# A windowed-attention and convolution kernel: the first MLP product in fp32, the normalised input in a ring of three, and a response stage that lags one strip more

## What is computed

```python
# layer 0, per window of 49 tokens, 3 heads
xn = layernorm(x, norm1)
q, k, v = split(xn @ qkv_w + qkv_b)
attn = softmax(q @ k.T * dh ** -0.5 + bias)
x = x + (attn @ v) @ proj_w + proj_b
h = gelu(layernorm(x, norm2) @ fc1_w + fc1_b)      # 48 -> 192
x = x + h @ fc2_w + fc2_b
# layer 1
y = layernorm(depthwise_conv7x7(x) + dw_b)
y = gelu(y @ w1 + b1)                              # 48 -> 192
gx = sqrt(sum over h, w of y * y)                  # per image and feature
nx = gx / (mean over features of gx + eps)
y = grn_g * (y * nx) + grn_b + y
out = x + y @ w2 + b2
```

## Time and profile before

| | |
|---|---|
| median of 3 runs | 2073.83 us (2071.69 to 2075.19) |
| profiled execution | 2077.34 us, span 2075.7 us |
| mean granted clock of TensorE | 0.946 |
| PE, PE weight loads | 1777.1 us (86%), 1065.6 us (51%) |
| VectorE (DVE) | 1508.5 us (73%) |
| ScalarE (ACT) | 1550.2 us (75%) |
| GpSimd (POOL) | 1174.7 us (57%) |
| first and last of the attention loop's `normalise1` | 80.5 and 1399.4 us |
| first and last output of the response stage | 1734.3 and 2060.2 us |

### The profile page before, as it was taken

The page is one execution under the profiler, slowest core; times in us unless marked ns, Lnnn a source line. Parts: engine busy times, 40 slices in busy tenths (PEclk is TensorE's granted clock), DMA queues, the critical chain, the costliest instruction groups (busy, mean ns, idle before and its releaser), DMA issues. The chain is left out here.

```text
span 2075.7 us, 90932 instructions
## 1 busy us (share of the span) xinstructions
PE 1777.1 (86%) x38074; PEld 1065.6 (51%) x38074; DVE 1508.5 (73%) x2014; ACT 1550.2 (75%) x2882; POOL 1174.7 (57%) x1048
## 2 busy tenths in 40 slices
PE   4989898989888898989898989874999959889884
PEld 2655555555555555555555555531788823223321
DVE  7687777878777777787777777534777757767772
ACT  3788888888888888888888888763566658777770
POOL 4676767777776767676767777731455611111121
PEclk9999999999999999999999999985899957889998
DMA  4334544343434343434434343312587769899983
GB/s 106 80 101 106 146 104 115 91 115 87 119 84 118 86 118 87 109 96 105 100 97 109 93 112 83 93 32 56 155 216 211 203 128 197 218 217 211 242 200 105
DMA packets 233223, 262.18 MB, mean 126 GB/s; under 512 B 167078, under 2 KB 179910, under 8 KB 232710
## 3 DMA queue, kind: packets, MB, share of 16 engines
q1 hardware_dynamic: 217478, 217.50, 43.1%
q0 software_dynamic: 15360, 39.08, 6.6%
HBM read 160.82 MB, written 80.88 MB: 116 GB/s over the span
## 5 line engine op out<-in xcount | busy, mean ns | idle before, releaser
L415 POOL TENSOR_TENSOR shift<-const_b,qmax 113x588 bf16<-113x588 bf16 x256 | 345.8, 1351 | 55.1 <-DVE qmax L510 54.9
L440 POOL TENSOR_TENSOR xl<-x 113x784 bf16<-113x784 f32 x64 | 136.7, 2136 | 263.8 <-DVE x L532 263.8
L1475 POOL DMA_DIRECT2D out_rolled<-r_OUT x128 | 64.3, 504 | 319.5 <-DVE r_OUT L1577 316.4
L510 DVE TENSOR_REDUCE qmax<-ps_s 113x12 f32<-113x588 f32 x256 | 194.7, 760 | 63.0 <-PE ps_s L890 63.0
L496 DVE TENSOR_TENSOR xh<-X,RS 113x784 f32<-113x784 f32 x64 | 229.1, 3580 | 2.9 <-DMA RS<-rs_scratch 2.1
L731 ACT ACTIVATE G<-ps_m 128x392 f32<-128x392 f32 x384 | 184.1, 498 | 50.9 <-PE ps_m L992 50.1
L699 ACT ACTIVATE P<-ps_t 113x588 f32<-113x588 f32 x256 | 171.9, 672 | 54.2 <-PE ps_t L942 53.5
L1323 PE MATMUL conv_ps<-xin,band_now 64*64 64x448 bf16 x2688 | 203.1, 364 | 4.1 <-DVE x_low L1225 4.1
L405 POOL TENSOR_TENSOR xhl<-xh 113x784 bf16<-113x784 f32 x64 | 203.4, 3178 | 2.2 <-DVE xh L550 2.2
L692 ACT COPY Uf<-ps_m 113x392 f32<-113x392 f32 x384 | 172.8, 485 | 30.9 <-PE ps_m L857 22.6
L502 DVE TENSOR_TENSOR Ul<-Uf 113x784 bf16<-113x784 f32 x192 | 182.6, 977 | 0.0
(11 more groups left out here) (240 smaller groups left out, 5267.3 us busy)
## 6 DMA issues: line engine op xcount, KB each, us to landing
xin<-rows_scratch SPq DMA_DIRECT2D x96, 236.0 KB, 3.8
XT<-x_tokens SPq DMA_DIRECT2D x64, 294.0 KB, 4.6
X<-x_windows SPq DMA_DIRECT2D x128, 147.0 KB, 2.9
RS<-rs_scratch SPq DMA_DIRECT2D x128, 147.0 KB, 3.4
XR<-x_windows SPq DMA_DIRECT2D x128, 147.0 KB, 3.7
x_scratch<-x SPq DMA_DIRECT2D x128, 147.0 KB, 3.9
y_scratch<-y POOLq DMA_DIRECT2D x96, 196.0 KB, 2.8
r_RS<-rs_scratch SPq DMA_DIRECT2D x128, 147.0 KB, 3.8
```

Of the source, the lines that this page charges most:

```text
L415: nc.gpsimd.tensor_tensor(shift[:, j % 2], e, m, ALU.mult).then_inc(S["md"], 1)
L440: nc.gpsimd.tensor_tensor(xl1[:], x1[:, r, :], x1m[0][:, r, :], ALU.subtract).then_inc(S["x1_lo"], 1)
L510: nc.vector.tensor_reduce(qmax[:, j % 2, :].rearrange("p (b n) -> p b n", b=2), ps_s[0:R, :, 0:2 * HQ].rearrange("p b (n t) -> p b n t", t ...
```

## The change

1. `fc1` of the attention stage multiplies fp32 weights with the fp32 normalised input, one product where three bf16 ones were; the split of its weights at setup, the tile `xhl1` and GpSimd's `low1` go, and `fc1` waits for `xh1` itself.
2. `xh0` and `xl0` get three slots (`HRING`); `normalise0(nx2)` moves on VectorE to the place between `divide(prv, 3)` and `first_residual(prv)`, `low0(nx2)` on GpSimd in front of `x1_low(prv)`; on SP `swap_halves` moves behind the loads of `X` and `RS`, `residual_load` behind `x2_store`.
3. In the response stage `LAG` is 11, the ring of `G` 14, `r_X` has three slots and is loaded a step earlier and ahead of `RS` and `Y`; the image's chain is spread over three steps and uses columns of `r_ps_m` instead of `r_ps_o`; ScalarE adds the epsilon to the mean; the hardware loop is written out.

```diff
@@ attention
-        w1_own = [sb(f"w1_own_{p}", [R, F1], BF16) for p in "hl"]
-        w1_part = [sb(f"w1_part_{p}", [R, F2], BF16) for p in "hl"]
+        w1_own = sb("w1_own", [R, F1])
+        w1_part = sb("w1_part", [R, F2])
...
-        xh0 = sb("xh0", [R, 2, STRIP])
-        xl0 = sb("xl0", [R, 2, STRIP], BF16)
+        xh0 = sb("xh0", [R, HRING, STRIP])
+        xl0 = sb("xl0", [R, HRING, STRIP], BF16)
...
             def step(s, image):
-                swap_halves(s.at(1))
                 x_load(s.at(2))
                 rs_load(s.at(2))
-                residual_load(s)
+                swap_halves(s.at(1))
                 tokens_load(s.at(TLEAD))
                 x2_store(s.at(-3), image)
+                residual_load(s)
                 rs_store(s.at(3))
...
-            def low1(s):
-
-                if s.real:
-                    wait(pool, S["xh1"], s.n + 1)
-                    wait(pool, S["f1"], 3 * s.n)
-                    nc.gpsimd.tensor_tensor(xhl1[:], xh1[:], xm1[0], ALU.subtract).then_inc(S["lo1"], 1)
...
                 make_shift(s, 2)
+                low0(nx2)
                 x1_low(prv)
-                low1(old)
                 make_shift(s, 3)
                 centre_tokens(s.at(4))
                 make_shift(nxt, 0)
                 squares_low(prv)
-                low0(nx2)
...
-                    wait(dve, S["st"], 4 * (s.n - 1))
-                    nc.vector.tensor_tensor(xh0[:, r, :], X[:, r, :], RS[:, r, :], ALU.mult).then_inc(S["xh0"], 1)
+                    wait(dve, S["st"], 4 * (s.n - 2))
+                    nc.vector.tensor_tensor(xh0[:, s.slot(HRING), :], X[:, r, :], RS[:, r, :], ALU.mult).then_inc(S["xh0"], 1)
...
                 divide(prv, 3)
+                normalise0(nx2)
                 first_residual(prv)
...
                 divide(s, 1)
-                normalise0(nx2)
                 query_max(nxt, 1)
...
                     if k == 0:
-                        wait(pe, S["lo1"], s.n + 1)
+                        wait(pe, S["xh1"], s.n + 1)
...
-                    for n, (w, m) in enumerate(((0, 0), (0, 1), (1, 0))):
...
+                    for b in range(2):
+                        for g in range(2) if k == 0 else (b,):
...
+                            ins = mm(out, weights, xh1[lo:lo + C + 1, cols], start=True, stop=True)
@@ response
-        RING = 2 * STRIPS
-        LAG = STRIPS + 2
+        RING = STRIPS + 6
+        SLOTS = 2 * STRIPS
+        LAG = STRIPS + 3
+        XRING = 3
...
-                nxt, old = s.at(2), s.at(-LAG)
+                nxt, old = s.at(2), s.at(1 - LAG)
+                if old.real:
...
+                    wait(sp, S["out_made"], old.n - XRING + 1)
...
                 nx2 = s.at(2)
-                respond(s.at(-LAG))
-                sum_squares(s.at(-2))
-                add_up(s.at(-LAG + 1))
+                sum_squares(s.at(-1))
+                add_up(s.at(-STRIPS))
                 finish(s.at(-LAG))
+                respond(s.at(-STRIPS - 2))
                 normalise(nx2)
...
                 features(s, 0)
                 features(s, 1)
-                norms_root(s.at(-LAG + 1))
                 features(s, 2)
+                keep_mean(s.at(-STRIPS - 1))
+                norms_root(s.at(-STRIPS))
                 sum_squares(s)
...
-                        wait(pe, S["ge"], 3 * (s.n - 1) + 1)
-                    elif t == 1:
-                        wait(pe, S["ge"], 3 * s.n)
+                    wait(pe, S["ge"], 3 * (s.n - 1) + t + 1)
...
                 fc1(s, 0)
-                respond(old, 1)
-                respond(old, 2)
                 fc2(old)
                 fc1(s, 1)
+                mean_of_norms(s.at(-STRIPS - 1))
+                pair_sums(s.at(-STRIPS))
                 fc1(s, 2)
-                respond(s.at(-LAG + 1), 0)
```

More of the change, by code:

```diff
@@ L849, in u_product @@
                     wait(pe, S["lo0"], s.n + 1)
-                    r = s.slot(2)
+                    r = s.slot(HRING)
                     for b in range(2):
@@ L1425, in halves, with steps @@
             return ap.rearrange("p (b n) -> p b n", b=2)
-        def steps(eng, step, last):
-            turns = max((N - RING - 2) // RING, 0)
-            for raw in range(-2, RING):
-                step(Strip(0, raw, N))
-            if turns:
-                with eng.Fori(0, turns) as i:
-                    for u in range(RING):
-                        step(Strip(RING // 4 * i, RING + u, N))
-            for raw in range(RING + RING * turns, last):
+        def steps(step, last):
+            for raw in range(-2, last):
                 step(Strip(0, raw, N))
@@ L1444, in step @@
             def step(s):
-                nxt, old = s.at(2), s.at(-LAG)
+                nxt, old = s.at(2), s.at(1 - LAG)
+                if old.real:
+                    if old.n == 0:
+                        wait(sp, S["cleared"], CLEARS)
+                    wait(sp, S["out_made"], old.n - XRING + 1)
+                    for g in range(2):
+                        sp.dma_start(X2[ROWB * g:ROWB * g + C, old.slot(XRING), :],
+                                     by_strip[0][old.n // STRIPS, old.n % STRIPS, g]
+                                     ).then_inc(x2_loaded[old.slot(XRING)], 16)
                 if nxt.real:
@@ L1454, in step @@
                                      ).then_inc(y_loaded[r], 16)
-                if old.real:
-                    if isinstance(old.n, int) and old.n == 0:
-                        wait(sp, S["cleared"], CLEARS)
-                    wait(sp, S["out_made"], old.n - 1)
-                    for g in range(2):
-                        sp.dma_start(X2[ROWB * g:ROWB * g + C, old.slot(2), :],
-                                     by_strip[0][old.n // STRIPS, old.n % STRIPS, g]
-                                     ).then_inc(x2_loaded[old.slot(2)], 16)
-            steps(sp, step, N + LAG)
+            steps(step, N + LAG)
         @block.gpsimd
@@ L1479, in step @@
                 store(s.at(-LAG))
-            steps(pool, step, N + LAG)
+            steps(step, N + LAG)
             for r in range(2):
@@ L1573, in finish @@
                     n = ROWB + C
-                    wait(dve, x2_loaded[s.slot(2)], 32 * (s.turn(2) + 1))
+                    wait(dve, x2_loaded[s.slot(XRING)], 32 * (s.raw // XRING + 1))
                     wait(dve, stored[s.slot(2)], 32 * s.turn(2))
@@ L1578, in finish @@
                         out=halves(OUT[:, s.slot(2), :]), in0=ps_o[0:n, :, 0:HALF], scalar=out_b[:, 0:1],
-                        in1=halves(X2[:, s.slot(2), :]), op0=ALU.add, op1=ALU.add).then_inc(S["out_made"], 1)
+                        in1=halves(X2[:, s.slot(XRING), :]), op0=ALU.add, op1=ALU.add).then_inc(S["out_made"], 1)
             def step(s):
                 nx2 = s.at(2)
-                respond(s.at(-LAG))
-                sum_squares(s.at(-2))
-                add_up(s.at(-LAG + 1))
+                sum_squares(s.at(-1))
+                add_up(s.at(-STRIPS))
                 finish(s.at(-LAG))
+                respond(s.at(-STRIPS - 2))
                 normalise(nx2)
-            steps(dve, step, N + LAG)
+            steps(step, N + LAG)
         @block.scalar
@@ L1624, in step @@
                 features(s, 1)
-                norms_root(s.at(-LAG + 1))
                 features(s, 2)
+                keep_mean(s.at(-STRIPS - 1))
+                norms_root(s.at(-STRIPS))
                 sum_squares(s)
-            steps(act, step, N + LAG)
+            steps(step, N + LAG)
         @block.tensor
@@ L1694, in fc2 @@
                     slot = s.raw % RING
+                    if s.raw % STRIPS == 0:
+                        wait(pe, S["w2_scaled"], 2 * (s.raw // STRIPS) + 2)
                     wait(pe, S["out_made"], s.n)
@@ L1712, in step @@
                 fc1(s, 0)
-                respond(old, 1)
-                respond(old, 2)
                 fc2(old)
                 fc1(s, 1)
+                mean_of_norms(s.at(-STRIPS - 1))
+                pair_sums(s.at(-STRIPS))
                 fc1(s, 2)
-                respond(s.at(-LAG + 1), 0)
-            steps(pe, step, N + LAG)
+            steps(step, N + LAG)
 def constants():
```

125 lines of the change are left out of this document (67 added, 58 removed).

## The result

The changed kernel takes **2099.74 us** (median of 4 runs, 2099.06 to 2103.93), the kernel before 2072.76 us (4 runs, 2071.44 to 2075.19) on the same chip: a ratio of 1.0133, with a 95% interval of 1.0115 to 1.0151. It is slower by 1.3%, where 0.5% faster was forecast. The profiled execution took 2103.93 us, its span is 2102.3 us. Of the runs behind this document one, of e13, was a slow one (2601.96 us at a mean granted clock of 0.65, where the other three had 0.92 to 0.93) and is left out of e13's time.

What follows compares the result with a forecast made beforehand. The attention step was taken as bound by PE's dense first half, then ScalarE, VectorE, GpSimd's `shift`, and fc1, GELUs and `fc2`. Attention + 28 and response - 38 gave - 10, so 2064 us against the 2073.8 median; range 2032 to 2092.

Steps and rivals of the forecast that it cites:

- The wait for `xhl`: Attention step: PE's 0.95 us wait at `fc1(old, 0)` becomes a longer wait at the shift; the step gains nothing.
- The longer ring: Attention step: fp32 results of fc1(1) and fc1(2) each come 0.24 us later, without slack: + 0.48 us a step.
- fill and drain: Attention stage outside its 62 full steps: - 2 us, since the last strip's low half goes.
- the term of + 28: Attention stage in all: 62 full steps x 0.48 = + 30 us, less 2 for fill and drain.
- The step that failed: Attention step: moving PE's 0.95 us wait from `fc1(old, 0)` to the shift was priced at no gain.
- six rivals: Six weighed outcomes for the whole kernel's time, from 2009 to 2152 us, with chances from 0.05 to 0.50.
- The response stage: Earlier `r_X` loads, spread chain, longer lag: - 38 us taken, bounds - 18 to - 49.
- image ends: Response stage: the extra time at each of six image ends falls from 7.0 to 2.9 us.
- no `fc2` of 2.88 us at image ends: Response stage, a sign that the forecast holds: the slow `fc2` first half at image ends disappears.
- Rival 3: Response stage: transfers bound it, every strip stays at 4.57 us; 2074 to 2094 us in all, chance 0.17.

Runs made afterwards that it cites:

- e13: The changed kernel with one extra fp32 product of constants on PE at the end of the step, behind `fc2`: 2185.6 us.
- e4: The changed kernel with three bf16 groups in `fc1`, the high half standing in for the low half, which GpSimd no longer makes: 2059.9 us.
- e5: The changed kernel with the first half of `fc1(old, 1)` computed once more than needed, in PE's gap in front of the shift: 2073.6 us.
- e12: The changed kernel with GpSimd's low half put back though nothing reads it; the fp32 product only waits for it: 2076.0 us.
- e10: The changed kernel with the first half of `fc1(old, 1)` computed once more than needed, directly behind the shift of quarter 3: 2120.8 us.

## Why the prediction was wrong

**The wait for `xhl`** (right for the usual step). It became a wait of 0.86 us at the shift, and e4 shows the step unchanged at 21.0 us; `xh0` takes 0.96 us in front of the first residual and cost nothing.

**The longer ring** (right for the step). 0.48 us a step was forecast, 0.49 measured (21.49 against 21.00), in e5 + 32.7 us over the loop. fc1's GELU starts 1.03 us after the fp32 round (832.55 to 833.58), as estimated from `fc2`. Only PE's own time for the pair was too low, 0.86 us a round instead of 0.71, and that was not in the ring. The 2 us taken off for fill and drain did not come: the term of + 28 is + 32.7.

**The step that failed** stands in the forecast as "So the 0.95 us becomes a longer wait one place on, and the step gains nothing from it." It was priced as if where PE waits didn't matter as long as the sum stays the same. Moved to 2 us in front of the wait for the GELU, it took the clock down, and that costs 26.9 us (e5; by the loop of e12, 1353.3 us with 2 falls left, it is 25.2). The term was put at nothing without a reason. With it the attention stage is + 59.6 us instead of + 28. None of the six rivals had the clock; I read it as 1.00 in the stage and took it for a constant. The range's upper end, 2092, was missed by 8 us for this term alone: without it the time would be 2073. From the forecast's - 10 to the measured + 26.6 us it is 36.6: 26.9 for the clock, 4.7 for the ring with fill and drain, 3.3 for the response stage and 1.7 for the rest.

**The response stage** (right in kind, 3 us too much): - 34.7 measured, - 38 forecast. But the two sizes in it were off and made up for each other. Over the first six images (48 distances), without the longest of each, outputs stand on average 4.92 us apart before and 4.47 after (4.57 and 4.37 in the forecast): I took one pair of neighbours for the usual one, and put what was missing in the image ends. The longest distance of an image went from 8.86 to 6.86 us on average, 2.0 less and not 4.1.

The clock was left out here too, and there it stood in the forecast's own rows. The `fc2` of 2.88 us at an image's end was read as a stall, but the same product takes 1.54 us at 1931.44 before, and over 1946 to 1951.5 us the mean granted clock is 0.73: it is TensorE at 1.2 GHz. Between the first and the last output the mean clock is 0.91 before and 0.97 after, which is 29 us of lost clock in 325.9 us against 9 in 287.6. By this estimate up to 20 of the 34.7 us may be the clock's, if PE set the pace in all of it; no run here separates them. The forecast's sign "no `fc2` of 2.88 us at image ends" did not come: one starts at 1942.74, in the fourth image's longest distance.

Rival 3, every strip at 4.57 us, fell: over 1850 to 2000 us the transfers moved 253 GB/s, before 225 over 1800 to 1950. The Trainium skill (DMA: Bandwidth & Descriptors, Specifications) denies the line rate to rows under 512 bytes. The rows of `r_Y` are as short as before, so what held this stage at 225 GB/s was not their length. That the transfers set part of the pace now is likely: their busy share over these 150 us rose from 0.94 to 1.02, and VectorE waits for `r_Y` 21 times, 17.1 us together and up to 2.6.

## What to carry to other kernels

A wait on PE that moves is not free even where the ring stays as long: look at the granted clock per step, and at how near the idle times of PE lie to each other, before and after. A length of step that has two values (here 21.49 and 22.77 us) under an unchanged order of work is its sign, and a harmless product in the gap prices it in one run. And when a wait moves one place on, go for what ends it there: the shift waited for a row maximum whose input was ready early, and moving that one instruction into idle time was worth 0.3 us a step with bf16 and, with the clock, 1.2 us with fp32.

## What the runs showed of the hardware

TensorE's clock falls to 1.2 GHz in the middle of a dense loop: no wait of PE in the step was longer than 1.03 us, and its work went on between them. With a wait of 0.86 us and one of 0.35 that ends 2 us later it fell in 16 of 60 steps. With the first wait filled by a product it fell in none (e5), with the first wait 2 us earlier in 2 (e12), both at the same length of step; with 0.66 us more between the two waits in 2 (e10), and with more work elsewhere in 34 (e13), both in a longer step. A fall cost 1.28 us, at times 2.9. The Trainium skill (TensorE: Matmul & The Clock Gate, Why this matters for your kernels) warns of long gaps between bursts of products, and this loop has none. The section "A second HAM failure mode: psum-queue depth-cycling" tells of a kernel in which TensorE "micro-idles between MM groups frequently enough" that its clock oscillates; the trace agrees that short waits can be enough, though here their place decides and not their number alone. Why it falls in some steps and not in their equal neighbours, and how near to each other the waits must lie, no run here shows.
